# Choosing the experts of the early batches with the eight-highest instruction, in two parts spread over more steps

## The chip, the cores and the metric

One NeuronCore of a Trainium2 chip runs the kernel. The metric is the device time in microseconds (us) of one execution. Engines are called TensorE (PE in the profile, PEld its weight loads), VectorE (DVE), ScalarE (ACT), GpSimd (POOL) and SyncE (SP, which issues most transfers).

## The reference

A transformer layer on 32 batches of 112 tokens with 256 channels. First x = x + tanh(g) * attention(layernorm(x), context), with 16 heads of 16 channels and a causal window. Then x = x + tanh(g') * ffn(layernorm(x)), where the ffn is a mixture of 32 experts. What matters here is how the experts are chosen:

```
h = gelu([x, six statistics of x] @ r1.T + b)      # 3584 tokens, 128 wide
probs = softmax(h @ r2.T)                          # 32 experts
topp, topi = top_k(probs, 2)                       # two per token, the lower index wins a tie
wnorm = topp / topp.sum()
score = where(expert is one of the two, probs, -inf)
idx = argsort(-score over the tokens)[:140]        # each expert takes its 140 best tokens
out[idx] += w * expert(x[idx])                     # and 16 adapters weighted alike
```

## The kernel before

**Groups and steps.** The attention runs in 8 groups (NG) of 4 batches (GB), T = 112 tokens each. Each group is a hand-written software pipeline of 16 steps (STEPS); a step is one unit of 4 heads of one batch. The function `group` exists once per engine, and its arguments say which parts a pass holds: `front` (projections of the next group), `own` (the scores of this group) and `prev` (what is left of the group before, and its layer norm and router input). `groups` calls it for the passes; the last two calls are body(7), with own and prev but no front, and body(8), with prev alone. Below, steps 0 to 15 are those of body(7), and steps 16 to 31 those of body(8).

**One pair of steps.** At an even step TensorE writes the scores of two units (L1366, L1371). VectorE takes the row maxima (L1241), ScalarE the exponentials of each unit (L1072), TensorE turns them (L1380), VectorE and ScalarE copy one unit each to SBUF (L1247, L1060), and TensorE multiplies with the values (`weigh`, L1399, at odd steps). Each batch also has its softmax denominators: a reciprocal (L1231), a spreading copy (L1079), two transposes (`turn_sums`, L1411), a copy (L1085), and the product that yields the attention of the batch (L1236, at steps 0, 4, 8, 12, 16 and 20). That product frees the bank for the next batch's `weigh`. Then come the output projection (item "O", L1331) and the residual (L1175). The steps of these are lags in a table (TURN, WEIGH, DENOM, SUMS, ATT); each engine executes its queue strictly in that written order, and semaphores join them.

**The router.** For each group of batches, the pass after it applies the second layer norm (L1199, step 8), makes statistics on VectorE (L1206 to L1222, steps 10 and 12) and on GpSimd (L961 to L966), turns the tokens (items "T", L1317), the statistics ("S", L1346) and multiplies with r1 ("H", L1350 and L1352). ScalarE stores the result in `hpre` (L1045).

**The early choices.** The 24 batches of groups 0 to 5 (EARLY) are chosen during body(7), in the room that the missing front leaves. ScalarE applies the gelu to six groups at step 0 (L448), with a load of another function table before and after. TensorE makes the logits (L486) of two groups each at steps 1, 2 and 6 (LOGITS), into bank BM[0], which holds 16 batches at a time. VectorE subtracts the row maximum (`shift_logits`, L528 and L529) for batches 0 to 15 at step 5 and for 16 to 23 at step 7 (SHIFTED), ScalarE takes one exponential of all 24 at step 8 (L1099), and `choose` (L532 to L563) follows on VectorE in ten parts, on all 24 batches, at steps 9 to 15 (CHOOSE). Each of its operations but a reciprocal reads 24 x 32 = 768 elements a partition. A maximum (L547), a comparison with it (L548), a product with the expert's rank (L550), a second maximum (L551) and a second comparison (L553) make one choice; L556 takes it out, and the same five make the second. Every operation waits for the one before through `link` (the helper `Chain`).

**The late ones.** Batches 24 to 27 get their gelu in body(8). After the attention (`routing_vector`, L578) the last 8 batches go through the same `shift_logits` and `choose` in one stretch, on 8 x 32 = 256 elements, with nothing else on VectorE; then TensorE turns the scores (L496), ScalarE copies them, and VectorE starts the search for each expert's 140th best score (L597 on). `token_weights` (L565) makes the experts' weights for the tokens, for the early ones at the last step of body(8).

**Keeping TensorE busy.** `keep_warm` (L406 to L409) issues products of 448 columns whose result nobody reads: 12, 18 and 2 of them at steps 7, 12 and 14 of body(8) (IDLE).

```
LOGITS = {1: (0, 1), 2: (2, 3), 6: (4, 5)}
CHOOSE = {9: (0, 1), 10: (2,), 11: (3,), 12: (4, 5), 13: (6,), 14: (7,), 15: (8, 9)}
```

Of the kernel before, what the change touches and what calls it, by code (L numbers as in the profile page):

```python
# [17 lines left out]
GB = 4  # L18
# [43 lines left out]
def table():  # L62

    t = np.zeros((128, TAB_COLS), np.float32)
    t[:, TAB["ident"]] = np.eye(128)
    half = DH // 2
    freq = (1.0 / 10000.0 ** (np.arange(half, dtype=np.float32) / half)).astype(np.float32)
    ang = np.arange(T, dtype=np.float32)[None, :] * freq[:, None]
    row = np.arange(128)
    t[:, TAB["cos"]] = np.cos(ang)[row % half]  # L70
    t[:, TAB["sin"]] = np.sin(ang)[row % half] * np.where(row % DH < half, -1.0, 1.0)[:, None]
    q = np.arange(T)
    t[:T, TAB["causal"]] = np.where(q[None, :] > q[:, None], -1e30, 0.0)
    t[:, TAB["rev"]] = NE - np.arange(NE)
    t[:, TAB["parity"]] = (row[:, None] // DH) % 2 == np.arange(2)[None, :]
    t[:, TAB["chunk"]] = (row[:, None] % NE) == (row[None, :] % NE)
    t[:, TAB["before"]] = t[:, TAB["chunk"]] * (row[:, None] < row[None, :])
    t[:, TAB["seek"]] = 1 + np.arange(PAD)
    t[:, TAB["first"]] = ((row // NE) * CHB * T - TOKENS)[:, None]
    t[:, TAB["share"]] = np.where(row == NST - 1, 1.0 / C, 1.0)[:, None]  # L80
    t[:, TAB["spare"]] = TOKENS + row[:, None] + HC * np.arange(2)[None, :]
    return t
# [86 lines left out]
GELU, GELU_TAIL, SHIFTED = 0, 5, (5, 7)  # L169
LOGITS = {1: (0, 1), 2: (2, 3), 6: (4, 5)}  # L170
CHOOSE = {9: (0, 1), 10: (2,), 11: (3,), 12: (4, 5), 13: (6,), 14: (7,), 15: (8, 9)}
# [46 lines left out]
def program(nc, d, ctx):  # L218
# [83 lines left out]
    prb, w0, w1, h1, h2 = (take(T, [NB, NE]) for _ in range(5))  # L302
    sc = take(T, [CHB, NCH, NE])
    sc_flat = sc.rearrange("p j c e -> p (j c e)")
    col = [take(T, [NB]) for _ in range(8)]
# [100 lines left out]
    def keep_warm(times, weights, data):  # L406

        for _ in range(times):
            nc.tensor.matmul(banks[BS[0]][0:T, 0:NT], weights, data, start=True, stop=True)  # L409
# [33 lines left out]
    EARLY = (NG - 2) * GB  # L443
    LATE = slice(EARLY, NB)

# [86 lines left out]
    def choose(dve, link, rows, part, count):  # L532

        n = rows.stop - rows.start
        c = [a[:, rows] for a in col]
        p, u, v = (a[:, rows, :] for a in (prb, w0, w1))
        rev = over_b(tab[0:T, TAB["rev"]], n)

        values, top, hit = (p, c[4], h1[:, rows, :]) if part < 5 else (u, c[5], h2[:, rows, :])
# [6 lines left out]
        elif part in (2, 6):  # L546
            link(nc.vector.tensor_reduce(top, values, X, ALU.max))  # L547
            link(nc.vector.tensor_tensor(v, values, over_e(top), ALU.is_equal))  # L548
        elif part in (3, 7):
            link(nc.vector.tensor_tensor(v, v, rev, ALU.mult))  # L550
            link(nc.vector.tensor_reduce(c[3], v, X, ALU.max))  # L551
        elif part in (4, 8):
            link(nc.vector.tensor_tensor(hit, v, over_e(c[3]), ALU.is_equal))  # L553
        elif part == 5:

            link(nc.vector.scalar_tensor_tensor(u, h1[:, rows, :], -2.0, p, ALU.mult, ALU.add))  # L556
        elif part == 9:

            link(nc.vector.tensor_tensor(v, h1[:, rows, :], h2[:, rows, :], ALU.add))
            for chunk in range(rows.start // CHB, rows.stop // CHB):  # L560
# [4 lines left out]
    def token_weights(link, rows):  # L565


        c = [a[:, rows] for a in col]
        link(nc.vector.tensor_tensor(c[6], c[4], c[5], ALU.add))
        link(nc.vector.reciprocal(c[7], c[6]))  # L570
        link(nc.vector.tensor_scalar(c[7], c[7], gates[0:T, 2:3], None, ALU.mult))
        nc.vector.tensor_tensor(c[4], c[4], c[7], ALU.mult)
        link(nc.vector.tensor_tensor(c[5], c[5], c[7], ALU.mult))
        nc.vector.tensor_tensor(prb[:, rows, :], h1[:, rows, :], over_e(c[4]), ALU.mult)
        link(nc.vector.tensor_tensor(w1[:, rows, :], h2[:, rows, :], over_e(c[5]), ALU.mult))
        nc.vector.tensor_tensor(wts[:, rows, :], prb[:, rows, :], w1[:, rows, :], ALU.add).then_inc(s_wts, 1)

    def routing_vector(dve, link):  # L578
# [9 lines left out]
        for part in range(10):  # L588
            choose(dve, link, LATE, part, 2)
# [410 lines left out]
    def _(act):  # L1000
# [53 lines left out]
        def group(g, par, front, own, prev, _=1):  # L1054
            for s in range(STEPS):
# [41 lines left out]
                if own and not front and s == SHIFTED[-1] + 1:  # L1097
                    act.wait_ge(s_sub, 2)
                    nc.scalar.activation(w0[:, 0:EARLY, :], w0[:, 0:EARLY, :], ACT.Exp).then_inc(s_e, 1)  # L1099
# [9 lines left out]
    def _(dve):  # L1109
# [116 lines left out]
        def group(g, par, front, own, prev, _=1):  # L1226
            for s in range(STEPS):
# [49 lines left out]
                if own and not front:  # L1277
# [5 lines left out]
                    for h, rows in enumerate((slice(0, 16), slice(16, EARLY))):  # L1283
                        if s == SHIFTED[h]:
                            shift_logits(dve, link, rows, BM[0], rows.stop // GB)
                    for part in CHOOSE.get(s, ()):
                        choose(dve, link, slice(0, EARLY), part, 1)
# [16 lines left out]
    def _(pe):  # L1304
# [114 lines left out]

        def group(g, par, front, own, prev, loads=1):  # L1420
            for s in range(STEPS):
                if own and s % 2 == 0:
                    scores(g, par, s)
                for back, u in unit_at(s, TURN, own, prev):
                    turn(g - back, u)
                for back, u in unit_at(s, WEIGH, own, prev):
# [19 lines left out]
                for early in LOGITS.get(s, ()) if own and not front else ():  # L1446
                    if early == 0:
                        pe.wait_ge(s_mf[0], len(FRONT) * NG)
                    if early == GB:
                        pe.wait_ge(s_sub, 1)  # L1450
                    logits(pe, slice(early * GB, (early + 1) * GB), BM[0], early % GB * GB * NE)
# [50 lines left out]
```

## Time and profile before

| what | us |
|---|---|
| median of 3 runs (818.8 to 819.85) | 819.19 |
| the profiled execution | 815.54 |
| its span, first to last instruction | 813.7 |
| VectorE busy in the span | 513.5 |
| TensorE busy in the span | 678.9 |

The attention takes the span's first 443 us, the routing runs to 538 us, and the experts take the rest. The profile was taken in one execution; its times are from the start of the span. A mean under an engine's name is that of single instructions, which overlap a little on VectorE and ScalarE: the end of one is still running when the next starts.

### The profile page before, as it was taken

How to read it: one execution, taken by the hardware profiler on the slowest of the kernel's cores; microseconds unless marked ns; L12 is line 12 of the kernel's file. 1: busy time of each engine (PE TensorE's matmuls, PEld its weight loads, DVE VectorE, ACT ScalarE, POOL GpSimd, SP SyncE). 2: the span in 40 equal slices, each digit the busy share in tenths (PEclk: the TensorE clock that was granted, in tenths of full speed). 3: DMA queues.
4: the chain of work that ended last, by engine and by line, in shares of the span. 5: the costliest groups of instructions: out<-in, count | busy, mean ns of one | idle time of the engine just before them, and what ended most of it. 6: DMA issues, size and time to landing. Idle time of an engine off the chain costs nothing.

```text
span 813.7 us, 17427 instructions
## 1 busy us (share of the span) xinstructions
PE 678.9 (83%) x5196; PEld 533.9 (66%) x5196; DVE 513.5 (63%) x1322; ACT 393.3 (48%) x1589; POOL 323.6 (40%) x339
## 2 busy tenths in 40 slices
PE   6889999999999999989776111059999999999993
PEld 3556666666666666657543100049999999999992
DVE  5665677867777786745976988944444444444541
ACT  1467686777768676876632364003222222222220
POOL 3343452534444363431102000034656565656542
PEclk9999999999999999997888555569999999999997
DMA  5600020202002020100003500017888898998931
GB/s 161 236 1 24 25 69 2 69 25 68 23 23 70 1 68 23 46 1 23 24 1 87 157 0 0 0 32 214 271 247 274 247 264 253 266 262 241 268 70 14
DMA packets 57422, 84.44 MB, mean 104 GB/s; under 512 B 11282, under 2 KB 28304, under 8 KB 57360
## 3 DMA queue, kind: packets, MB, share of 16 engines
q1 hardware_dynamic: 47168, 73.04, 27.4%
q0 software_dynamic: 9216, 9.76, 7.6%
q10 hardware_dynamic: 976, 0.96, 0.4%
q8 instruction: 20, 0.33, 0.2%
q14 instruction: 42, 0.34, 0.1%
HBM read 71.04 MB, written 12.69 MB: 103 GB/s over the span
## 4 chain that ended last, share of the span: by engine, by line
PE 60%; DVE 19%; ACT 13%; issue 4%; DMA 1%; POOL 1%; ACTq 1%; DVEq 0%; POOLq 0%
PE pair L797 19%; PE bank L807 10%; ACT arena L1072 6%; PE pair L1371 6%; DVE arena L1241 5%; PE bank L1399 3%; PE pair L1380 3%; PE pair L1366 3%; DVE arena L658 3%; PE bank L1338 3%; PE bank L1326 2%; PE bank L1331 2%; PE bank L817 2%; ACT arena L477 2%; ACT arena L1027 1%
## 5 line engine op out<-in xcount | busy, mean ns | idle before, releaser
L1072 ACT ACTIVATE arena<-pair,arena 112x112 f32<-112x112 f32 x512 | 175.5, 365 | 81.1 <-DVE arena L1241 77.6
L797 PE MATMUL pair<-arena,we 128*128 128x140 f32 x1024 | 138.2, 283 | 0.8 <-ACT arena L718 0.6
L761 DVE SCALAR_TENSOR_TENSOR arena<-arena,pair 128x140 f32<-128x140 f32 x160 | 47.6, 298 | 137.0 <-ACT arena L726 137.0
L703 POOL DMA_INDIRECT rows_out<-arena,slot_row x64 | 94.4, 1475 | 91.0 <-DVE arena L750 75.2
L797 PEld LDWEIGHTS pair<-arena,we 128*128 128x128 f32 x1024 | 128.4, 190 | 1.9 <-issue 1.9
L726 ACT ACTIVATE arena<-pair 128x140 f32<-128x140 f32 x160 | 45.9, 287 | 147.4 <-PE pair L797 147.4
L694 POOL DMA_INDIRECT arena<-rows,slot_row x64 | 62.5, 977 | 121.2 <-issue 121.2
L1072 ACT ACTIVATION_READ_ACCUMULATOR arena<-pair,arena 112x1 f32 x512 | 109.9, 215 | 0.0
L1241 DVE TENSOR_REDUCE arena<-pair 112x8 f32<-112x896 f32 x64 | 69.2, 1081 | 25.7 <-PE pair L1371 25.0
L807 PE MATMUL bank<-arena,we 128*128 128x140 f32 x512 | 83.3, 286 | 0.0
L1380 PEld LDWEIGHTS pair<-tab,arena 112*112 112x112 f32 x512 | 53.2, 137 | 31.3 <-issue 28.5
L1380 PE MATMUL pair<-tab,arena 112*112 112x112 f32 x512 | 73.0, 270 | 0.0
L1399 PE MATMUL bank<-arena 112*32 112x112 f32 x1024 | 66.0, 273 | 6.4 <-DVE arena L1236 6.4
L807 PEld LDWEIGHTS bank<-arena,we 128*128 128x128 f32 x512 | 69.8, 190 | 0.0
L930 POOL TENSOR_TENSOR arena<-arena,tab 128x448 f32<-128x448 f32 x30 | 34.0, 1133 | 87.6 <-DVE we L1140 87.4
L1371 PE MATMUL pair<-arena 32*112 32x224 f32 x512 | 65.8, 374 | 0.0
L1399 PEld LDWEIGHTS bank<-arena 112*32 112x32 f32 x1024 | 49.7, 114 | 17.1 <-DVE arena L1236 6.8
L1326 PE MATMUL bank<-arena 128*128 128x448 f32 x128 | 58.6, 586 | 0.8 <-ACTq L1022 0.5
L1371 PEld LDWEIGHTS pair<-arena 32*112 32x112 f32 x512 | 40.8, 173 | 19.5 <-issue 18.0
L1366 PE MATMUL pair<-arena 112*112 112x448 bf16 x128 | 42.1, 375 | 7.0 <-ACT arena L1060 5.2
L766 DVE TENSOR_TENSOR arena<-arena,pair 128x140 f32<-128x140 f32 x128 | 38.4, 300 | 5.0
L1236 DVE TENSOR_TENSOR arena<-bank,arena 128x224 f32<-128x224 f32 x32 | 12.6, 393 | 43.3 <-ACT arena L1085 40.4
(192 smaller groups left out, 1183.7 us busy)
## 6 DMA issues: line engine op xcount, KB each, us to landing
we<-w_experts_in SPq DMA_DIRECT2D x192, 256.0 KB, 4.3
wa<-w_adapters_in SPq DMA_DIRECT2D x16, 384.0 KB, 5.7
arena<-ctx_in SPq DMA_DIRECT2D x8, 448.0 KB, 4.4
arena<-x_in SPq DMA_DIRECT2D x8, 448.0 KB, 3.8
rows_out<-arena SPq DMA_DIRECT2D x8, 448.0 KB, 3.3
rows<-arena SPq DMA_DIRECT2D x8, 448.0 KB, 3.4
arena<-rows,slot_row POOLq DMA_INDIRECT x64, 4.4
rows_out<-arena,slot_row POOLq DMA_INDIRECT x64
```

The lines of the kernel that those rows point to most:

```text
L694: nc.gpsimd.indirect_dma_start(xr[e % 4][:, h, :], None, d["rows"], bass.IndirectOffsetOnAxis(ap=slot_row[:, h, e:e + 1], axis=0)).then_in ...
L703: nc.gpsimd.indirect_dma_start(d["out"], bass.IndirectOffsetOnAxis(ap=slot_row[:, h, e:e + 1], axis=0), yr[e % 2][:, h, :], None, compute_ ...
L761: signal(dve, nc.vector.scalar_tensor_tensor(gs[m % 2], th[m % 2], 1.0, banks[m % 4][:, 0:CAP], ALU.add, ALU.mult), s_gs, n + 1)
L797: last = nc.tensor.matmul(banks[m % 4][:, part * CAP:(part + 1) * CAP], w[:, col0:col0 + 128], xet[j % 2][:, c, :], start=(c == 0), stop=( ...
L807: last = nc.tensor.matmul(banks[5 + o][:, 0:CAP], w[:, col0 + o * 128:col0 + (o + 1) * 128], hh[j % 2][:, k, :], start=(k == 0), stop=(k = ...
L1072: last = nc.scalar.activation(pr[s % 2][:, j, :], banks[BS[s % 4]][0:T, j * T:(j + 1) * T], ACT.Exp, bias=nmx[s // 2 % 2][:, s % 2, j:j + ...
L1241: nc.vector.tensor_reduce(nmx[s // 2 % 2], pairs[s // 2 % 2][0:T, :, 0:HU * T].rearrange("p u (h k) -> p u h k", h=HU), X, ALU.max, negate ...
L1326: last = nc.tensor.matmul(out[:, 0:NT], w[:, c, j * 128:(j + 1) * 128], src[:, c, :], start=(c == 0), stop=(c == 1))
L1366: nc.tensor.matmul(banks[BS[(s + i) % 4]][0:T, 0:HU * T], identb, causalb.unsqueeze(1).to_broadcast([T, HU, T]), start=True, stop=False)
L1371: last = nc.tensor.matmul(banks[BS[(s + i) % 4]][0:T, 2 * t * T:2 * (t + 1) * T], qt[par][rows, t, b * T:(b + 1) * T], kz[b % 2][rows, t, ...
L1380: last = nc.tensor.transpose(banks[BS[u % 4]][0:T, j * T:(j + 1) * T], pr[u % 2][:, j, :], ident[0:T, 0:T])
L1399: last = nc.tensor.matmul(banks[BO][rows, j // 2 * T:(j // 2 + 1) * T], vx[par][:, b * (NH // 2) + h // 2, 2 * (j % 2):2 * (j % 2) + 2, :] ...
```

## The change

The two highest of 32 values come from one instruction per batch, `nc.vector.max`, which writes the eight highest values of each partition in order (112 x 32 in, 112 x 8 out), into `top8` and `key8`. The choice goes in nine parts: sum and reciprocal (0), product (1), the eight highest of each batch's probabilities (2), their difference from the second highest (3), a key of 1 - e/32 where that isn't negative (4), plus 1 where it is positive (5), the eight highest of the keys (6), a comparison with the second of them (7), and the scores (8). `token_weights` multiplies the scores by one factor for each token.

The early batches go in two parts, 0 to 15 and 16 to 23, over steps 3 to 15 and 17 to 21; the tail of the choices runs in body(8). The logits of groups 4 and 5 move from step 6 to step 4. TensorE gets 7 unread products ahead of the logits at step 1, 2 ahead of those at step 4 and 4 at step 15, into bank BM[0].

```
-GELU, GELU_TAIL, SHIFTED = 0, 5, (5, 7)
-LOGITS = {1: (0, 1), 2: (2, 3), 6: (4, 5)}
-CHOOSE = {9: (0, 1), 10: (2,), 11: (3,), 12: (4, 5), 13: (6,), 14: (7,), 15: (8, 9)}
+GELU, GELU_TAIL = 0, 5
+LOGITS = {1: (0, 1), 2: (2, 3), 4: (4, 5)}
+EARLY_ROWS = (slice(0, 16), slice(16, 24))
+SHIFTED, RAISED = (3, 9), (4, 10)
+PARTS = 9
+CHOOSE = {5: ((0, 0), (0, 1)), 7: ((0, 2),), 9: ((0, 3),), 11: ((0, 4),), 13: ((0, 5),), 15: ((0, 6),),
+          16: ((0, 7), (0, 8)), 17: ((1, 0), (1, 1), (1, 2)), 19: ((1, 3), (1, 4), (1, 5)), 20: ((1, 6),),
+          21: ((1, 7), (1, 8))}
+IDLE_LOGITS, WITH_LOGITS = 7, 2
+IDLE_LAST = {15: 4}
...
         elif part in (2, 6):
-            link(nc.vector.tensor_reduce(top, values, X, ALU.max))
-            link(nc.vector.tensor_tensor(v, values, over_e(top), ALU.is_equal))
-        elif part in (3, 7):
-            link(nc.vector.tensor_tensor(v, v, rev, ALU.mult))
-            link(nc.vector.tensor_reduce(c[3], v, X, ALU.max))
-        elif part in (4, 8):
-            link(nc.vector.tensor_tensor(hit, v, over_e(c[3]), ALU.is_equal))
+            values, out = (prb, top8) if part == 2 else (w0, key8)
+            for b in range(rows.start, rows.stop):
+                last = nc.vector.max(out[:, b, :], values[:, b, :])
+            link(last)
+        elif part == 3:
+            link(nc.vector.tensor_tensor(v, p, second(top8), ALU.subtract))
+        elif part == 4:
+            link(nc.vector.scalar_tensor_tensor(u, v, 0.0, over_b(tab[0:T, TAB["rev"]], n), ALU.is_ge, ALU.mult))
         elif part == 5:
-            link(nc.vector.scalar_tensor_tensor(u, h1[:, rows, :], -2.0, p, ALU.mult, ALU.add))
-        elif part == 9:
-            link(nc.vector.tensor_tensor(v, h1[:, rows, :], h2[:, rows, :], ALU.add))
-            for chunk in range(rows.start // CHB, rows.stop // CHB):
+            link(nc.vector.scalar_tensor_tensor(u, v, 0.0, u, ALU.is_gt, ALU.add))
+        elif part == 7:
+            link(nc.vector.tensor_tensor(v, u, second(key8), ALU.is_ge))
+        elif part == 8:
+            for chunk in chunks:
                 at = slice(chunk * CHB, (chunk + 1) * CHB)
                 last = nc.vector.tensor_tensor(sc[:, :, chunk, :], prb[:, at, :], w1[:, at, :], ALU.mult)
             link(last)
...
     def token_weights(link, rows):
-        link(nc.vector.tensor_tensor(c[6], c[4], c[5], ALU.add))
-        link(nc.vector.reciprocal(c[7], c[6]))
-        link(nc.vector.tensor_scalar(c[7], c[7], gates[0:T, 2:3], None, ALU.mult))
-        nc.vector.tensor_tensor(c[4], c[4], c[7], ALU.mult)
-        link(nc.vector.tensor_tensor(c[5], c[5], c[7], ALU.mult))
-        nc.vector.tensor_tensor(prb[:, rows, :], h1[:, rows, :], over_e(c[4]), ALU.mult)
-        link(nc.vector.tensor_tensor(w1[:, rows, :], h2[:, rows, :], over_e(c[5]), ALU.mult))
-        nc.vector.tensor_tensor(wts[:, rows, :], prb[:, rows, :], w1[:, rows, :], ALU.add).then_inc(s_wts, 1)
+        link(nc.vector.tensor_tensor(c[0], top8[:, rows, 0], top8[:, rows, 1], ALU.add))
+        link(nc.vector.reciprocal(c[3], c[0]))
+        link(nc.vector.tensor_scalar(c[3], c[3], gates[0:T, 2:3], None, ALU.mult))
+        for chunk in range(rows.start // CHB, rows.stop // CHB):
+            at = slice(chunk * CHB, (chunk + 1) * CHB)
+            last = nc.vector.tensor_tensor(wts[:, at, :], sc[:, :, chunk, :], over_e(col[3][:, at]), ALU.mult)
+        last.then_inc(s_wts, 1)
...
-                if own and not front and s == SHIFTED[-1] + 1:
-                    act.wait_ge(s_sub, 2)
-                    nc.scalar.activation(w0[:, 0:EARLY, :], w0[:, 0:EARLY, :], ACT.Exp).then_inc(s_e, 1)
+                if own and not front and s in RAISED:
+                    h = RAISED.index(s)
+                    act.wait_ge(s_sub, h + 1)
+                    rows = EARLY_ROWS[h]
+                    nc.scalar.activation(w0[:, rows, :], w0[:, rows, :], ACT.Exp).then_inc(s_e, 1)
...
+        def fill_in(times):
+            keep_warm(times, identb, causalb.unsqueeze(1).to_broadcast([T, HU, T]), BM[0])
+
         def group(g, par, front, own, prev, loads=1):
             for s in range(STEPS):
                 if own and s % 2 == 0:
                     scores(g, par, s)
                 for back, u in unit_at(s, TURN, own, prev):
                     turn(g - back, u)
+                if own and not front and s in IDLE_LAST:
+                    pe.wait_ge(s_sub, 2)
+                    fill_in(IDLE_LAST[s])
...
                     if early == 0:
                         pe.wait_ge(s_mf[0], len(FRONT) * NG)
-                    if early == GB:
+                        fill_in(IDLE_LOGITS)
+                    elif early == GB:
                         pe.wait_ge(s_sub, 1)
+                        fill_in(WITH_LOGITS)
```

## Rows read from the trace of the kernel before

**Rows 1.** Busy time by stretch: PE, PEld, DVE, ACT, POOL, PEclk, DMA share, GB/s.
```profile
356.00:376.00 20.00, 17.46 (x118) 12.70 (x116) 4.59 (x8) 14.52 (x52) 0.93 (x1) 0.74 0.00 1
376.00:389.90 13.90, 12.91 (x123) 9.34 (x119) 11.11 (x26) 9.30 (x46) 2.21 (x3) 1.00 0.12 34
389.90:417.70 27.80, 19.28 (x135) 13.03 (x135) 26.48 (x48) 15.93 (x70) 3.56 (x6) 0.85 0.06 18
...
417.70:428.00 10.30, 8.87 (x54) 6.00 (x54) 4.36 (x14) 2.61 (x4) 0.13 (x1) 0.74 0.05 16
```

**Rows 2.** Chain of waits, steps 10 to 17: start, us, what.
```profile
397.87 0.96 DVE arena L547
...
417.71 0.40 DVE arena L1236
...
418.16 1.71 PE bank L1399 x16
```

**Rows 3.** VectorE's timeline, 386 to 428 us: start, us, engine, line, operation, shapes.
```profile
386.17 0.39 DVE L1236 TENSOR_TENSOR arena<-bank,arena 128x224 f32<-128x224 f32 x1 [0.97 <-ACT arena L1085]
...
392.37 1.03 DVE L1241 TENSOR_REDUCE arena<-pair 112x8 f32<-112x896 f32 x1
...
402.13 1.08 DVE L1241 TENSOR_REDUCE arena<-pair 112x8 f32<-112x896 f32 x1
...
410.53 1.03 DVE L1241 TENSOR_REDUCE arena<-pair 112x8 f32<-112x896 f32 x1
...
427.14 0.18 DVE L1191 BATCH_NORM_AGGREGATE arena<-arena 112x2 f32<-112x6 f32 x1
```

**Rows 4.** Groups of VectorE's instructions, shapes apart, whole span: busy, mean ns.
```profile
L547 DVE TENSOR_REDUCE arena<-arena 112x24 f32<-112x768 f32 x2 | 1.9, 953 | 0.1
L528 DVE TENSOR_REDUCE arena<-bank 112x16 f32<-112x512 f32 x1 | 0.7, 692 | 0.2 <-DVE arena L1187 0.2
L547 DVE TENSOR_REDUCE arena<-arena 112x8 f32<-112x256 f32 x2 | 0.8, 419 | 0.1
L1187 DVE BATCH_NORM_AGGREGATE arena<-arena 112x2 f32<-112x6 f32 x24 | 2.5, 161 | 1.2 <-DVE arena L1184 0.9
```

**Rows 5.** VectorE's timeline: three small independent instructions in a row.
```profile
379.09 0.31 DVE L1187 BATCH_NORM_AGGREGATE arena<-arena 112x2 f32<-112x6 f32 x3
```

**Rows 6.** TensorE's timeline in steps 1 to 4 and at step 12.
```profile
362.76 1.73 PE L486 MATMUL bank<-r2t,hpre 128*112 128x32 f32 x16 [1.83 <-ACT hpre L448]
...
365.97 1.84 PE L1371 MATMUL pair<-arena 32*112 32x224 f32 x8
...
368.52 3.06 PE L486 MATMUL bank<-r2t,hpre 128*112 128x32 f32 x16
...
375.25 1.01 PE L1371 MATMUL pair<-arena 32*112 32x224 f32 x8
...
390.25 0.40 PE L1366 MATMUL pair<-arena 112*112 112x448 bf16 x1 [1.26 <-ACT arena L1060]
```

**Rows 7.** Busy time by microsecond, columns of rows 1: where the granted clock changes.
```profile
365.00:366.00 1.00, 0.58 (x3) 0.20 (x3) 0.00 (x0) 0.98 (x2) 0.00 (x0) 0.50 0.00 0
...
375.00:376.00 1.00, 1.00 (x9) 0.63 (x8) 0.39 (x1) 0.00 (x0) 0.00 (x0) 0.90 0.00 0
...
392.00:393.00 1.00, 1.00 (x10) 0.99 (x8) 0.96 (x3) 0.86 (x2) 0.00 (x0) 0.63 0.07 24
...
436.00:437.00 1.00, 1.00 (x5) 0.57 (x4) 1.00 (x7) 0.00 (x0) 0.33 (x1) 0.68 0.00 0
```

**Rows 8.** Timelines of ScalarE and TensorE from 414 us.
```profile
414.97 0.39 ACT L1085 COPY arena<-bank 128x224 f32<-128x224 f32 x1
...
433.25 5.26 PE L409 MATMUL pair<-arena 112*112 112x448 bf16 x18
```

**Rows 9.** Chain of waits in the choice of the late batches.
```profile
447.08 0.43 DVE arena L542
...
454.25 1.77 PE pair L496 x8
```

More of the change, by code:

```diff
@@ L73, in table @@
     t[:T, TAB["causal"]] = np.where(q[None, :] > q[:, None], -1e30, 0.0)
-    t[:, TAB["rev"]] = NE - np.arange(NE)
+    t[:, TAB["rev"]] = 1 - np.arange(NE) / NE
     t[:, TAB["parity"]] = (row[:, None] // DH) % 2 == np.arange(2)[None, :]
@@ L301, in program @@
     used[0] = 0
-    prb, w0, w1, h1, h2 = (take(T, [NB, NE]) for _ in range(5))
+    prb, w0, w1 = (take(T, [NB, NE]) for _ in range(3))
+    top8, key8 = (take(T, [NB, 8]) for _ in range(2))
     sc = take(T, [CHB, NCH, NE])
     sc_flat = sc.rearrange("p j c e -> p (j c e)")
-    col = [take(T, [NB]) for _ in range(8)]
+    col = [take(T, [NB]) for _ in range(4)]
     assert used[0] <= free_early
@@ L404, in groups, with keep_warm @@
         body(NG, 0, False, False, True)
-    def keep_warm(times, weights, data):
+    def keep_warm(times, weights, data, bank=BS[0]):
         for _ in range(times):
-            nc.tensor.matmul(banks[BS[0]][0:T, 0:NT], weights, data, start=True, stop=True)
+            nc.tensor.matmul(banks[bank][0:T, 0:NT], weights, data, start=True, stop=True)
     PIECE = 512
@@ L443, in program @@
     EARLY = (NG - 2) * GB
+    assert EARLY_ROWS[-1].stop == EARLY
     LATE = slice(EARLY, NB)
@@ L536, in choose @@
         p, u, v = (a[:, rows, :] for a in (prb, w0, w1))
-        rev = over_b(tab[0:T, TAB["rev"]], n)
-        values, top, hit = (p, c[4], h1[:, rows, :]) if part < 5 else (u, c[5], h2[:, rows, :])
+        second = lambda a: over_e(a[:, rows, 1])
+        chunks = range(rows.start // CHB, rows.stop // CHB)
         if part == 0:
@@ L587, in routing_vector @@
         shift_logits(dve, link, LATE, BS[0], EARLY // GB + 1)
-        for part in range(10):
-            choose(dve, link, LATE, part, 2)
+        for part in range(PARTS):
+            choose(dve, link, LATE, part, 3)
         dve.sem_inc(s_scr, 1)
@@ L1282, in group @@
                             dve.wait_ge(done, value)
[L1283 to L1287, printed above, removed]
+                    if s in SHIFTED:
+                        rows = EARLY_ROWS[SHIFTED.index(s)]
+                        shift_logits(dve, link, rows, BM[0], rows.stop // GB)
+                if not front:
+                    for h, part in CHOOSE.get(s if own else s + STEPS, ()):
+                        choose(dve, link, EARLY_ROWS[h], part, h + 1)
         dve.wait_ge(s_gate, 1)
```

## The prediction

> **What bounds the kernel now.** I read the stretches first. From 389.9 to 417.7 us, steps 9 to 15, VectorE is busy 26.5 of 27.8 us and TensorE 19.3 [rows 1]: the only part of the attention in which VectorE is the bound. The chain of waits says the same: from 397.87 to 417.71 us it runs through nothing but VectorE, over the choice (L547 to L562), to the product L1236 on which TensorE's `weigh` starts at 418.16 [rows 2]. The rhythm shows what that costs. The maxima L1241 of steps 10, 12 and 14 begin at 392.37, 402.13 and 410.53 [rows 3], 9.8 and 8.4 us apart; ahead of the choice steps 4 and 8 took some 5 us a pair (376 to 389.9 us, TensorE busy 12.9 of 13.9 [rows 1]).
>
> A second loss lies in steps 1 to 4. ScalarE has the gelus, TensorE waits 1.83 us, and its granted clock falls to 0.50 (1.2 GHz) at 365 us and is back at 375 [rows 6, 7]. There eight products of the scores take 1.84 us and later 1.01, and 16 logits 3.06 against 1.73 just before [rows 6].
>
> The third place is the choice of the last 8 batches, 447.08 to 454.25 us, all of it on VectorE, and TensorE waits for its end [rows 9].
>
> **Prices on VectorE.** An operation on 768, 512 and 256 elements takes 0.95, 0.69 and 0.42 us [rows 4]; with the 0.04 us between linked ones I take 0.99, 0.73 and 0.46. The two ends give 1.04 ns an element. No row has the eight-highest instruction. It reads 32 elements, 0.033 us at that rate. Three small independent instructions took 0.31 us together at 0.161 each, so 0.075 from start to start [rows 4, 5]. I take 0.11 us for each, since the eight highest of the batches are independent too. The lower end is 0.08 (only the spacing). The upper end is a small instruction's full 0.161 [rows 4], the 0.033 and nearly nothing of overlap, 0.20. So eight take 0.9 us with their link, sixteen 1.8; at the upper end 1.6 and 3.2.
>
> The row speaks for overlap. The Trainium skill, VectorE: DVE Perf Modes, in its section on the TRN2 errata, speaks against the change: each instruction on SBUF pays a fixed latency, whatever its size, and work should be cut in tiles of 512 elements or more; it has measured about 150 cycles of it. By that an estimate of the instruction is 0.19 us and the sum below is that of the second rival. That the latency isn't paid in full between independent instructions is what the three small ones show here.
>
> **The change, part by part.**
>
> 1. *Steps 8 to 16.* Before, the choice holds fourteen operations on 768 elements (14 x 0.99), a reciprocal (about 0.3) and three score products on 256 (together 1.1): 15.3 us. After, steps 9 to 15 hold the shift of 8 batches (2 x 0.46), three operations on 16 batches (3 x 0.73) and sixteen eight-highest (1.8): 4.9 us. L1236 of step 8 begins at 386.17 and that of step 16 at 417.71 [rows 2, 3], 31.5 us. VectorE alone would need 31.5 - 15.3 + 4.9 = 21.1 us. But other work now ends last. Step by step: the maxima of step 10 at 391.4 (5 us behind those of step 8, TensorE's pace). Those of step 12 at 397.8: other work filled 392.37 to 397.87, 5.5 us [rows 2, 3], and 0.73 and the reciprocal or product ahead of the maxima join it. Those of step 14 at 403.0: from 8.4 us go four operations, 4.0, and 0.73 comes. From there the chain of exponentials, copy, transposes and L1085 took 410.53 to 415.36 in the trace [rows 3, 8], 4.8 us. It gives L1236 at 408.0 instead of 417.71: **-9.7 us**. Late next are ScalarE's L1085, and VectorE's sixteen, which end at 406.8; they have 1.2 us to spare. The four unread products at step 15 stand ahead of `weigh` and H, 4 x 0.19 us (part 6). TensorE would reach the sums' transposes at about 406.7, and ScalarE copies them at 407.6. Hidden; without that cover 0.8 us.
>
> 2. *Steps 3 to 8.* The first shift goes to step 3, where VectorE is idle (busy 4.6 of 20 us [rows 1]); queued behind its wait for the logits is only step 4's product, which comes later. Sum, reciprocal and product at step 5 take 1.7 us where the shift took 1.6. The logits of step 4, with two unread products, put 2.1 us in front of `weigh` and O, and the maxima of step 6 some 1.5 us later; step 6 loses as much, and with ScalarE's exponential of all 24 batches out of step 8 the maxima of step 10 come at 391.4 all the same, not at 392.37. Cost nothing beyond part 1. Without that cover it would be 1.5 us.
>
> 3. *Steps 16 to 22.* New on VectorE: 0.73 + 0.76, then 0.69 + 0.46 + 0.9, then 3 x 0.46, then 0.9, then 0.96: 6.8 us. In this stretch it was busy 4.4 of 10.3 us [rows 1], so 0.9 us don't fit, and since the new work stands in the queue ahead of the reciprocal of step 18 and of the product of step 20, another 1.2 us of its idle time is of no use: L1191, which ends the second layer norm's statistics at 427.3 [rows 3], comes 11.7 us after step 16's product instead of 9.6. **+2.1 us.** GpSimd's root and the following norm wait for it.
>
> 4. *The late choice.* Before 7.17 us [rows 9]. After: seven operations on 256 elements (7 x 0.46), a reciprocal (0.23) and twice 0.9: 5.25 us. **-1.9 us.** `token_weights` gets shorter, beside the transposes and copies; nothing. No transfer is added or moved past a queue.
>
> 5. *TensorE's clock in steps 1 to 4.* Seven unread products take 1.3 us of the 1.83 it waits [rows 6]. From 365.97 to 376.26 us, 10.3 us, TensorE works without a gap, nearly all at the lower clock; by the pairs 1.84 to 1.01 and 3.06 to 1.73 [rows 6] it would be 0.56 as long, 4.5 us less, if the clock stayed at 2.4 GHz. I take 0: at 392 us it fell behind a wait of only 1.26 us with TensorE busy on both sides [rows 6, 7], and the rest of the wait and the short logits remain. Ends: +0.8 (the seven at the lower clock), -4.5.
>
> 6. *The 18 unread products of step 28* end last at their place: 5.26 us from 433.25 [rows 8], with the clock rising at 436.7 [rows 7], so nine at each level: 9 x a + 9 x 2a gives a = 0.195 us. All at 1.2 GHz they are 7.0, all at 2.4 GHz 3.5. I take no change; ends +1.7 and -1.7.
>
> Sum: -9.7 + 2.1 - 1.9 = -9.5 us. Against the profiled execution's 815.54 that is 806.0. The median of the runs stands 3.65 us above that execution; I carry the difference over: 819.19 - 9.5 = **809.7 us**.
>
> **The rivals.**
>
> *A, the clock holds in steps 1 to 4* (part 5 at its end): 809.7 - 4.5 = 805.2. For it, two thirds of the wait are filled. Against it, the fall at 392.
>
> *B, the eight-highest instruction costs 0.20 us.* The late choice gives back 2 x 0.7; steps 17 and 20 the same 1.4; step 7 has 3.2 us instead of 1.8 ahead of step 8 and delays it 1.3; step 15 eats its 1.2 and 0.2 more: 809.7 + 4.3 = 814.0. The page named above gives this.
>
> *C, TensorE takes the bound over.* With VectorE relieved, steps 9 to 16 keep TensorE at it nearly all the time (19.3 us busy [rows 1] plus the fill); if a pair takes 5.5 us instead of 5.1 and the 18 products run at 1.2 GHz: 3 x 0.4 + 1.7, 812.6.
>
> *D, slower: the eight-highest instruction runs on its own at 0.35 us.* Place: 16 late, 16 in steps 17 and 20, 16 in step 7, 16 in step 15. Each 0.1 us more costs 5 to 6 us, so from 0.28 us on the gain of 9.5 is gone; at 0.35 the time is 823. The smallest reduction and statistics read above take under 0.2 beyond their elements [rows 4], so this is unlikely.
>
> *E, the relief doesn't arrive*, since another wait of these steps was as late as VectorE: only the late choice gains, 817.3. Against it, TensorE waits for L1236 in both places.
>
> **How the numbers follow.** Forecast 52%, A 18%, B 12%, C 12%, D 3%, E 3%. The forecast's own range is 808 to 811.5. The range that holds 8 in 10 reaches from just under A to just over B and leaves out D, E and the far ends: 804.8 to 814.5. About 0.2% is what a measurement of this kernel can tell from no change. Faster than that are the forecast, A, B, C and E: 0.95; slower D: 0.03; the rest within it, 0.02.
>
> **What the changed profile would show.** Part 1: the maxima of steps 10, 12 and 14 some 5 to 6.5 us apart, and L1236 of step 16 led by ScalarE's L1085, 8 to 10 us earlier against step 8's. Part 3: the same lines 11 to 12 us from step 16's product to the last aggregate. Part 4: 5.2 us from the late sum to the transposes, and eight instructions in 0.9 us. Part 5: granted clock 0.50 for some 10 us behind the gelus. Wrong it would be with eight of them in over 1.3 us, with gaps over 7 us still between those maxima, or with a clock of 1.00 from 365 to 375 us.

## The result and the profile after

| | us |
|---|---|
| before, median of 18 runs (814.95 to 822.39) | 818.86 |
| changed, median of 18 runs (808.84 to 819.33) | 815.87 |
| ratio, with its 95% interval | 0.9959 (0.994 to 0.9978) |
| changed, the profiled execution | 816.06 |
| its span | 814.3 |

The change gains 3 us by the medians, 1.8 to 4.9 us by the interval of the ratio, not 9.5. Two things in the table are worth more than its median: the changed kernel's quickest runs are 6 us below the quickest before, and its runs scatter by 10 us. Single executions of three kernels below stand apart with another granted clock (818.52 and 1391.63 us of two changed kernels, 1186.83 us of the kernel before); the medians and ratios leave them out.

The page of the changed kernel: share of the span by engine, and TensorE's granted clock in 40 slices.

```profile
span 814.3 us, 17505 instructions
PE 682.5 (84%) x5209; PEld 536.7 (66%) x5209; DVE 508.7 (62%) x1371; ACT 394.2 (48%) x1590; POOL 323.4 (40%) x339
...
PEclk8999999999999999995887555579999999999997
```

VectorE lost 4.8 us of work. The clock stands at its lower level in the nineteenth slice (366 to 387 us, from step 2 on), where before it was at 7 tenths.

VectorE's timeline of the changed kernel, the maxima of steps 0, 4, 6, 8, 10, 12 and 14 (L1254), the product of steps 8 and 16 (L1249), the eight-highest instructions (L562), and the aggregate that ends the tail (L1204). Start, us, engine, line, operation, idle time before.

```profile
356.59 1.09 DVE L1254 TENSOR_REDUCE arena<-pair 112x8 f32<-112x896 f32 x1 [0.49 <-PE pair L1385]
...
375.60 1.09 DVE L1254 TENSOR_REDUCE arena<-pair 112x8 f32<-112x896 f32 x1 [1.78 <-PE pair L1385]
...
385.88 1.09 DVE L1254 TENSOR_REDUCE arena<-pair 112x8 f32<-112x896 f32 x1 [5.08 <-PE pair L1385]
...
388.95 1.59 DVE L562 MAX8 arena<-arena 112x8 f32<-112x32 f32 x16 [0.15 <-DVE arena L1204]
390.88 0.39 DVE L1249 TENSOR_TENSOR arena<-bank,arena 128x224 f32<-128x224 f32 x1 [0.34 <-DVE arena L562]
391.19 1.08 DVE L1254 TENSOR_REDUCE arena<-pair 112x8 f32<-112x896 f32 x1
...
396.05 1.03 DVE L1254 TENSOR_REDUCE arena<-pair 112x8 f32<-112x896 f32 x1
...
402.58 1.08 DVE L1254 TENSOR_REDUCE arena<-pair 112x8 f32<-112x896 f32 x1
...
408.74 1.09 DVE L1254 TENSOR_REDUCE arena<-pair 112x8 f32<-112x896 f32 x1 [0.91 <-PE pair L1385]
...
414.27 0.39 DVE L1249 TENSOR_TENSOR arena<-bank,arena 128x224 f32<-128x224 f32 x1 [1.78 <-issue]
...
426.07 0.18 DVE L1204 BATCH_NORM_AGGREGATE arena<-arena 112x2 f32<-112x6 f32 x1
```

The timeline shows two opposite things. From step 8's product to step 16's it is now 23.4 us, before 31.5 [rows 2, 3]: the gaps of 9.8 and 8.4 us are 6.5 and 6.2. But the maxima of step 6 come 10.3 us behind those of step 4, with VectorE idle for 5.08 us and waiting for TensorE. Before, these were 5 us apart, and step 8 began 28.3 us behind step 0 instead of 34.6. The kernel before, the maxima of steps 0, 4, 6 and 8:

```profile
358.15 1.09 DVE L1241 TENSOR_REDUCE arena<-pair 112x8 f32<-112x896 f32 x1 [0.50 <-PE pair L1371]
...
376.34 1.09 DVE L1241 TENSOR_REDUCE arena<-pair 112x8 f32<-112x896 f32 x1 [0.95 <-PE pair L1371]
381.31 1.03 DVE L1241 TENSOR_REDUCE arena<-pair 112x8 f32<-112x896 f32 x1
...
386.47 1.08 DVE L1241 TENSOR_REDUCE arena<-pair 112x8 f32<-112x896 f32 x1
```

TensorE's timeline in that hole, steps 1 to 6.

```profile
359.21 1.50 PE L420 MATMUL bank<-arena 112*112 112x448 bf16 x7
361.11 1.76 PE L498 MATMUL bank<-r2t,hpre 128*112 128x32 f32 x16 [0.40 <-ACT hpre L460]
...
364.41 1.84 PE L1385 MATMUL pair<-arena 32*112 32x224 f32 x8
366.18 0.99 PE L1394 MATMUL pair<-tab,arena 112*112 112x112 f32 x4
366.96 3.06 PE L498 MATMUL bank<-r2t,hpre 128*112 128x32 f32 x16
...
373.69 1.84 PE L1385 MATMUL pair<-arena 32*112 32x224 f32 x8
375.46 0.99 PE L1394 MATMUL pair<-tab,arena 112*112 112x112 f32 x4
376.25 0.95 PE L420 MATMUL bank<-arena 112*112 112x448 bf16 x2
377.00 3.06 PE L498 MATMUL bank<-r2t,hpre 128*112 128x32 f32 x16
...
382.41 2.05 PE L1345 MATMUL bank<-arena 128*112 128x256 f32 x4
```

And busy time by stretch with the granted clock (behind the length: PE, PEld, DVE, ACT, POOL, then PEclk).

```profile
355.00:362.00 7.00, 6.60 (x55) 4.70 (x55) 2.18 (x4) 5.46 (x19) 0.00 (x0) 1.00 0.00 1
...
364.00:384.00 20.00, 20.00 (x107) 15.73 (x108) 8.60 (x18) 10.40 (x46) 0.94 (x1) 0.50 0.00 1
...
401.00:408.00 7.00, 6.73 (x38) 4.64 (x38) 6.56 (x16) 3.97 (x20) 2.70 (x5) 0.53 0.01 2
```

The clock fell at 364 us in spite of the seven unread products, and it stayed at 1.2 GHz for 20 us; before it was 10 [rows 7]. The moved logits (377.00, 3.06 us where they take 1.7 at full clock) lie in the middle of it, on TensorE's path, 20 of 20 us busy.

The end of the late choice, VectorE's timeline.

```profile
449.42 0.84 DVE L562 MAX8 arena<-arena 112x8 f32<-112x32 f32 x8
...
456.53 0.63 DVE L608 TENSOR_SCALAR arena<-arena 128x896 int32<-128x896 int32 x1 [4.06 <-DMA arena<-search_in]
```

SyncE's timeline in the same stretch: start, us, queue, line, operation.

```profile
450.28 0.65 SPq L910 DMA_DIRECT2D arena<-search_in  x1
452.50 0.34 SPq L912 DMA_DIRECT2D rows<-wts  x1
```

The choice itself is as short as forecast, 446.01 to 451.25 us. But the first digit of the search (L608) waits 4.06 us for the search table, which SyncE issues behind 13 loads of weights at 450.28 and which lands 6.2 us later. From the end of the attention (VectorE's first MEMSET behind it, at 442.15 and before at 443.22) to that digit it is 14.4 us, before 13.9. From the sum that opens the choice (L555, at 446.01, before L542 at 447.08) to the digit it is 10.5 us, before 10.0.

### The profile page after: what moved, and what is told of

It is laid out like the page before. It is cut to its first block, busy times and chain, and to the rows that moved or that the text cites. A ratio compares the mean times of both kernels' runs of the same rounds, so it can differ in the third digit from the quotient of the medians.

```text
span 814.3 us, 17505 instructions
## 1 busy us (share of the span) xinstructions
PE 682.5 (84%) x5209; PEld 536.7 (66%) x5209; DVE 508.7 (62%) x1371; ACT 394.2 (48%) x1590; POOL 323.4 (40%) x339
## 4 chain that ended last, share of the span: by engine, by line
PE 61%; DVE 17%; ACT 12%; issue 4%; DMA 2%; SPq 1%; POOL 1%; ACTq 0%; DVEq 0%; POOLq 0%
PE pair L808 19%; PE bank L818 10%; PE pair L1385 6%; ACT arena L1083 6%; DVE arena L1254 4%; PE pair L1394 3%; PE bank L1413 3%; PE pair L1380 3%; DVE arena L669 3%; PE bank L1352 3%; PE bank L1345 2%; PE bank L1340 2%; PE bank L828 2%; PE bank L1364 2%; PE bank L1331 1%
## 5 line engine op out<-in xcount | busy, mean ns | idle before, releaser
L1254 DVE TENSOR_REDUCE arena<-pair 112x8 f32<-112x896 f32 x64 | 69.4, 1084 | 30.8 <-PE pair L1385 30.0
L1413 PE MATMUL bank<-arena 112*32 112x112 f32 x1024 | 64.2, 268 | 0.3 <-DVE arena L1249 0.3
L1340 PE MATMUL bank<-arena 128*128 128x448 f32 x128 | 56.1, 565 | 0.6 <-ACTq L1033 0.3
L1260 DVE COPY arena<-pair 112x448 f32<-112x448 f32 x64 | 39.4, 616 | 0.4 <-PE pair L1394 0.4
```

Of the source, the lines that this page charges most:

```text
L1254: nc.vector.tensor_reduce(nmx[s // 2 % 2], pairs[s // 2 % 2][0:T, :, 0:HU * T].rearrange("p u (h k) -> p u h k", h=HU), X, ALU.max, negate ...
L1340: last = nc.tensor.matmul(out[:, 0:NT], w[:, c, j * 128:(j + 1) * 128], src[:, c, :], start=(c == 0), stop=(c == 1))
L1413: last = nc.tensor.matmul(banks[BO][rows, j // 2 * T:(j // 2 + 1) * T], vx[par][:, b * (NH // 2) + h // 2, 2 * (j % 2):2 * (j % 2) + 2, :] ...
```

## The experiments

Each kernel is compared with the kernel before on the same chip. The medians of the kernel before differ by up to 3 us between chips, so the ratios are what compares; behind each stands its 95% interval. "Steps 0 to 8" is the time from the maxima of step 0 to those of step 8 in the profile. Each profile is of one execution only, and it isn't always a typical one.

**Each suspected loss alone.**

The table's transfer first:

```
-        load_pair(1, 1)
         nc.sync.dma_start(srt, d["search"]).then_inc(s_dig, 16)
+        load_pair(1, 1)
```

> The changed kernel, with the transfer of the search table issued ahead of the 13 expert loads at the end of the attention instead of behind them. Theory (the late choice's gain is eaten by this transfer): the table lands before 450 us of the profile instead of 456.5, the first digit follows ScalarE's copies at about 2.4 us behind the place where it stood (456.53 becomes about 454.1), and the median falls by 2 to 2.5 us below that of the changed kernel, to 813.5. Rival (SyncE's loads are what matters, or another wait is as late): no change, 815.9, and VectorE's first digit still at 14.4 us behind the attention's end.

Measured: median 812.12, ratio 0.993 (0.9905 to 0.9955), against 0.9959 for the changed kernel, some 2.4 us better, though the two intervals overlap. The first digit now follows ScalarE's copy, 12.7 us behind the attention's end instead of 14.4, and 8.15 us behind the sum that opens the choice instead of 10.5.

> The kernel before with the same swap of the two transfers. Theory: there the table lands 0.2 us ahead of ScalarE's copy, so nothing is gained: 818.9, ratio 1.000 within 0.002. Rival (the order of the transfers is worth something by itself, whatever the choice costs): 816.5, ratio 0.997.

Measured: 817.96, ratio 1.0007 (0.9987 to 1.0027). Alone the order of the transfers gains nothing: from the sum to the digit it is 10.0 us as without it. The table became a bound only when the choice got shorter than it.

The logits back:

```
-LOGITS = {1: (0, 1), 2: (2, 3), 4: (4, 5)}
+LOGITS = {1: (0, 1), 2: (2, 3), 6: (4, 5)}
```

> The changed kernel with the logits of groups 4 and 5 back at step 6; all else as changed. Theory (the logits at step 4 fall into the time in which the clock is low after the gelus, and keep it low for steps 4 and 5): granted clock back at 1.00 some 10 us after its fall and not 20, maxima of step 8 about 29 us behind those of step 0 instead of 34.6, median 810 to 813, and fewer runs above 816. Rival (the clock's course is chance, and the place of the logits costs nothing): 815.9 with the same spread.

Measured: 810.68 (807.77 to 812.47), ratio 0.9931 (0.9911 to 0.995), 2.3 us better than the changed kernel; the two intervals just touch. The profile fell on the quickest of the six runs. Steps 0 to 8 take 28.6 us instead of 34.6, and the clock is back some 10 us behind its fall:

```profile
363.00:373.00 10.00, 9.40 (x53) 7.46 (x53) 3.40 (x5) 7.12 (x30) 0.94 (x1) 0.51 0.01 2
373.00:375.00 2.00, 2.00 (x16) 1.25 (x15) 0.87 (x2) 0.14 (x1) 0.00 (x0) 0.90 0.00 0
375.00:400.00 25.00, 22.06 (x204) 15.70 (x204) 22.90 (x67) 19.32 (x91) 5.52 (x9) 1.00 0.13 38
```

With the clock up, the rest of the forecast stands in this kernel's timelines: step 8's product at 384.57, step 16's at 406.40, 21.8 us, and the last aggregate at 418.11. ScalarE's copy (L1096) ends at 406.31, just ahead of step 16's product.

```profile
384.57 0.39 DVE L1249 TENSOR_TENSOR arena<-bank,arena 128x224 f32<-128x224 f32 x1 [0.34 <-DVE arena L562]
...
405.92 0.39 ACT L1096 COPY arena<-bank 128x224 f32<-128x224 f32 x1
406.40 0.39 DVE L1249 TENSOR_TENSOR arena<-bank,arena 128x224 f32<-128x224 f32 x1 [1.25 <-issue]
...
418.11 0.18 DVE L1204 BATCH_NORM_AGGREGATE arena<-arena 112x2 f32<-112x6 f32 x1
```

No unread products (`IDLE_LOGITS, WITH_LOGITS = 0, 0` and `IDLE_LAST = {}`):

> The changed kernel without its 13 unread products (7, 2 and 4). Theory (they do not hold the clock: in the profile it fell at 364 us in spite of them): 815.9, within 1 us, clock low from 364 us on for as long as with them. Rival (they hold it in the quick half of the runs, 808.8 to 812.4): no run below 813, median 818.

Measured: 809.78 (807.35 to 814.47), ratio 0.9934 (0.9905 to 0.9962). Neither expectation: by the median it gains as much as moving the logits back (the interval still holds the changed kernel's 0.9959), and in the profile, again of the quickest run, the clock was back after 10 us although the logits stood at step 4. So the loss may lie in the unread products, or in them and the moved logits together, as well as in the logits, and this profile already shows that logits at step 4 don't always mean a long low stretch.

**The mends together, beside the changed kernel again.**

> The changed kernel, nothing edited, beside the three below on one chip, as their measure. Theory (the course of the clock in steps 1 to 6 makes two kinds of runs): ratio to before 0.996 again, runs from some 3 us below the median to 3 us above, and a mean clock of the run that goes with its time.

Measured: 815.15 (808.62 to 817.96), ratio 0.9958 (0.9931 to 0.9985), the first measurement again. Its profile fell on its quickest run: clock low from 365.5 to 372.3 us only, steps 0 to 8 in 28.3 us. Taken together the changed kernel's 30 runs go from 808.62 to 819.33, 12 of them below 813.5, and their time goes with the mean granted clock, at a correlation of -0.94 (0.914 at 808.84, 0.898 at 819.33). That clock is a mean over the whole execution, and the kernel before has the same correlation on this chip (-0.95), so it doesn't show that steps 1 to 6 are what differs.

> The changed kernel with both mends: the logits of groups 4 and 5 at step 6, and the search table's transfer ahead of the expert loads. Theory (two separate losses): the gains add, 2.3 us and 2.4 us below the changed kernel of the same chip, ratio to before 0.990, which is the forecast's 9.5 us less about 1. Rival (one of the two stands for the other): ratio 0.993 like either alone.

Measured: 811.24 (807.37 to 814.43), ratio 0.991 (0.988 to 0.994). Against the changed kernel on the same chip (0.9958) that is 3.9 us, clear of the noise. The theory's 0.990 and the rival's 0.993 both lie in the interval, so whether the two gains add in full isn't shown.

> The run before it (both mends) without the 13 unread products. Theory (they do nothing where the logits are at step 6, since the clock falls at the same place with and without them): the same within 0.1%. Rival (each unread product before step 4 stands in TensorE's way while its clock is low, as the run without them at step 4 hinted): 1 to 2 us faster still, ratio 0.988. Other rival (they hold the clock in some runs): slower by 1 to 2 us.

Measured: 809.4 (807.42 to 811.75), ratio 0.9898 (0.9862 to 0.9934). The interval holds the run before it and the first rival's 0.988; no use of the 13 products shows here.

Four more, in TensorE's second wait of step 1:

```
                     logits(pe, slice(early * GB, (early + 1) * GB), BM[0], early % GB * GB * NE)
+                    if early == 1:
+                        fill_in(4, BM[2])
```

> Both mends, and 4 more unread products right behind the logits of step 1, in the second wait, into bank BM[2]. Theory (the clock falls since TensorE waits and then has only narrow logits; with the second wait filled too it may stay): if it holds, steps 0 to 4 take 14 us instead of 18.2 and the ratio goes to 0.985. Rival (the narrow products of 32 columns and scores of 32 rows are what lets it fall): it falls at the same place, ratio 0.990.

Measured: 805.7 (803.68 to 806.06), ratio 0.9841 (0.9807 to 0.9875). That is 5.5 us better than without the four. In the profile the clock stays: steps 0 to 4 take 14.0 us, steps 0 to 8 24.4. TensorE's timeline:

```profile
361.28 1.50 PE L420 MATMUL bank<-arena 112*112 112x448 bf16 x7
363.18 1.76 PE L498 MATMUL bank<-r2t,hpre 128*112 128x32 f32 x16 [0.40 <-ACT hpre L460]
364.77 0.95 PE L420 MATMUL bank<-arena 112*112 112x448 bf16 x4
365.56 0.77 PE L1380 MATMUL pair<-arena 112*112 112x448 bf16 x2
366.26 1.01 PE L1385 MATMUL pair<-arena 32*112 32x224 f32 x8
...
367.63 1.67 PE L498 MATMUL bank<-r2t,hpre 128*112 128x32 f32 x16
```

Its stretches, with the granted clock behind the five engines:

```profile
362.00:373.00 11.00, 10.58 (x95) 7.94 (x92) 4.06 (x7) 10.27 (x36) 0.94 (x1) 1.00 0.01 2
373.00:383.00 10.00, 9.11 (x87) 6.70 (x86) 8.82 (x34) 7.52 (x37) 2.00 (x3) 1.00 0.16 46
```

The products stand in a wait of 0.78 us; the scores behind them still start with ScalarE's copy, and take 1.01 us instead of 1.84.

**What each part is worth.**

> The quickest version so far (both mends, 7 and 4 unread products at step 1), with the logits of groups 4 and 5 back at step 4. Theory (their place costs only where the clock is low): the clock stays, and the ratio is 0.984 to 0.986, as with step 6. Rival (they cost by their order, 2.1 us in front of the scores of step 6): ratio 0.987 or more.

Measured: 806.47 (804.59 to 808.91, five runs), ratio 0.9888 (0.986 to 0.9917) of the kernel before. In the profile the clock stays up, and steps 0 to 8 take 25.1 us instead of 24.4: the order of the logits costs 0.7 us at full clock, where the changed kernel's profile was 6 us longer than with the logits at step 6. The ratio lies on the rival's side (0.987 or more), and the theory's 0.984 to 0.986 only touches the interval, so the runs as a whole leave room for a larger cost than 0.7 us.

The kernel before with the same 7 and 4 products and nothing else:

> The kernel before with nothing but 7 and 4 unread products at step 1. Theory (the low clock of steps 1 to 4 is a loss of its own, 4.2 us from the scores of step 2 to those of step 4, and it passes on): clock at 1.00 through steps 1 to 4, ratio 0.995. Rival (VectorE, the bound from step 9 on, swallows it): ratio 0.999.

Measured: 811.51, ratio 0.9937 (0.9913 to 0.996). The low clock of steps 1 to 4 was a loss of its own, by the medians larger than the gain of the whole change as made (5 us against 3; the intervals overlap). In the profile steps 0 to 4 take 14.0 us; there the clock falls later, from 379 to 389 us, and that execution took 816.41.

The eight-highest instruction for the late batches alone, in the kernel before:

> The kernel before with the eight-highest instruction for the late 8 batches alone; the early ones and the schedule as before. Theory (the search table's transfer is as late as the old choice): the choice takes 5.2 us instead of 7.2, but the first digit starts only 0.2 us or so sooner behind the attention's end, ratio 0.9995. Rival (my forecast's -1.9 us arrives): ratio 0.9977.

Measured: 816.73, ratio 0.9992 (0.9969 to 1.0015). The choice is 1.9 us shorter, and nothing measurable comes of it, but the interval holds the rival too. In the profile the digit waits 2.29 us for the table and starts 13.3 us behind the attention's end.

> The same with the search table's transfer ahead of the expert loads. Theory: the 1.9 us arrive, the first digit starts 12.0 us behind the attention's end instead of 13.9, ratio 0.9977. Rival (something else is as late as the table): ratio 1.000.

Measured: 816.71, ratio 1.0002 (0.9986 to 1.0018). The first digit starts 12.7 us behind the attention's end, in the profile of the kernel before with the table first 14.6. So the 1.9 us reach the digit; the absolute 12.0 and 13.9 us of the expectation don't recur, since in this profile the logits ahead of the choice ran at the lower clock. Yet the median has none of it, and the interval leaves out the theory's 0.9977.

**The same questions in the quickest version.**

> The quickest version again (logits at step 6, table first, 7 and 4 unread products at step 1), as the measure of the three beside it on one chip: ratio 0.984 to 0.987, scatter of the runs under 4 us.

Measured: 805.19 (802.94 to 808.57), ratio 0.9867 (0.9836 to 0.9898). The ratio is as expected, the scatter isn't: 5.6 us, not under 4.

> That version with the old ten-part choice and the old weights for the last 8 batches. Theory (the late choice's 1.9 us arrive once the table doesn't wait): 1.9 us slower than the quickest version, median difference 1.5 to 2.5 us. Rival (they are lost again before the experts, in the clock's rise or elsewhere): within 0.5 us of it.

Measured: 805.78 (803.46 to 811.69), ratio 0.9879 (0.9842 to 0.9916). The difference of medians is 0.6 us, near the rival's 0.5, but each interval reaches some 3 us to either side and settles nothing between 0 and 1.9 us. The profiles show both sides. The digit starts 1.9 us later with the old choice (14.6 against 12.7), but the experts' first 24 products take 3.10 us, as in the kernel before, and 4.76 with the new choice, since the clock is up 1.2 us ahead of them in the one and 3.4 us behind their start in the other. TensorE's timeline at the experts' start, with the old late choice:

```profile
533.79 3.10 PE L848 MATMUL pair<-arena,we 128*128 128x140 f32 x24 [0.57 <-ACT arena L769]
```

The same with the new one, in the profile of the first quickest version:

```profile
532.40 4.76 PE L808 MATMUL pair<-arena,we 128*128 128x140 f32 x24 [0.57 <-issue]
```

> That version without the 2 unread products at step 4 and the 4 at step 15. Theory (they fill waits in which the clock doesn't fall anyway, and steps 12 to 16 hang on ScalarE): the same within 0.5 us. Rival (the four at step 15 keep the clock): 1 to 2 us slower, with the clock at 0.50 in steps 15 to 18.

Measured: 805.0 (801.32 to 811.11), ratio 0.9878 (0.9837 to 0.992). The same by the median, with a scatter of 9.8 us; in the profile the clock in steps 4 to 15 didn't fall without them. (The two products go with the logits, so in this version they stood at step 6.)

> That version without the 7 unread products at step 1, with the 4 behind the logits alone. Theory (both waits have to be filled): the clock falls some 5 to 9 us behind the maxima of step 0 again, 4 us slower. Rival (the second wait alone decides): as quick as the quickest version.

Measured: 810.22 (807.82 to 812.16), ratio 0.9928 (0.99 to 0.9957), 5 us slower. The clock falls and stays low for 20 us:

```profile
363.00:383.00 20.00, 20.00 (x105) 14.85 (x104) 8.54 (x18) 12.22 (x50) 0.93 (x1) 0.50 0.00 1
```

Both waits of step 1 have to be filled. The change filled the first alone, which shows no gain. The profiles of all kernels agree: in the six with both waits filled the clock stays up through steps 1 to 4, and in the other twelve it falls.

**How long the low stretch lasts.** This is the stretch behind step 0 in those twelve profiles, sorted by the place of the logits of groups 4 and 5. "First" and "second" are the unread products in the two waits of step 1.

| kernel | logits at | first, second | clock low, us | steps 0 to 8, us |
|---|---|---|---|---|
| changed | 4 | 7, 0 | 20 | 34.6 |
| changed, table first | 4 | 7, 0 | 17 | 33.0 |
| changed, measured again | 4 | 7, 0 | 7 | 28.3 |
| changed, no unread products | 4 | 0, 0 | 10 | 29.1 |
| changed, logits back | 6 | 7, 0 | 10 | 28.6 |
| both mends | 6 | 7, 0 | 10 | 28.5 |
| both mends, no unread products | 6 | 0, 0 | 14 | 29.5 |
| quickest version without the seven | 6 | 0, 4 | 20 | 32.6 |
| before | 6 | 0, 0 | 10 | 28.3 |
| before, table first | 6 | 0, 0 | 10 | 28.2 |
| before, new late choice | 6 | 0, 0 | 17 | 30.3 |
| before, new late choice, table first | 6 | 0, 0 | 10 | 28.3 |

One kernel has 7 and 20 us, and stretches of 17 and 20 us also come with the logits at step 6. So the profiles don't show that the moved logits lengthen the stretch. They do show what the logits cost inside it: in a stretch of 17 or 20 us steps 0 to 8 are 2.7 and 2.0 us longer with the logits at step 4 than at step 6, in one of 10 us some 0.5 to 0.9 us, and at full clock 0.7 us.

## Why the prediction was wrong, point by point

**Prices: right.** Eight of the new instructions took 0.84 us and sixteen 1.59, against 0.9 and 1.8 with their link. Independent ones follow each other every 0.1 us. The Trainium skill (VectorE: DVE Perf Modes, section on the TRN2 errata) has a fixed latency of about 150 cycles for each instruction; an estimate with it in full each time is 1.5 us for eight. The trace, with 0.84 us, disagrees for a row of independent small instructions.

**Part 1, -9.7 us: right where the clock was up.** The kernel with the logits at step 6 has 21.8 us between the two products, the number forecast, and ScalarE's copy ends last, 0.1 us ahead of the second, as forecast. The changed kernel has 21.8 us too in its second profile; in the first it has 23.4, where the clock was at 0.53 from 401 to 408 us.

**Part 2, "cost nothing beyond part 1": wrong, the step that failed.** I moved the logits to step 4 with two unread products and priced their order at full clock, with 1.5 us as the bound, to be made good by step 10. At full clock it is 0.7 us in the profiles. But my own part 5 had the clock low from 365 to 375 us, and step 4 begins at its end: if the stretch lasts longer than the 10 us of the one profile I had, the moved logits and their two products cost nearly twice as much, as does all of TensorE's work beside them. With the logits back the ratio falls by 0.28%, 2.3 us, and with both mends by 3.9 us. In the changed kernel's first profile steps 0 to 8 are 6.3 us longer than before, but most of that is the long low stretch itself. I treated its length as given; it is 7 to 20 us in the profiles, and why it is long in one execution and short in the next stays open, as does the share of the unread products: by the median, leaving them out gained as much as moving the logits back.

**Part 3, +2.1 us: right in size.** It was 2.4 in the changed kernel (414.27 to 426.25 us, before 9.6) and 2.3 with the logits at step 6. No run shows what it costs the whole.

**Part 4, -1.9 us: right for the choice, wrong for the path, the second step that failed.** 5.24 us instead of 7.17. What I wrote of the transfers, that none is moved past a queue, was true and beside the point: one was already as late as the old choice. In the kernel before, the table landed at 456.85 us (issued at 451.45, 5.4 us on its way), 0.2 us ahead of the end of ScalarE's copy at 457.01, and the wait was invisible, because that copy ended last. In the changed kernel the wait comes last, and its size varies: from the sum that opens the choice to the digit the four profiles with the table behind the loads have 10.5, 9.1, 8.4 and 10.3 us, those with the table first 8.15 us. So the wait takes 0.2 to 2.4 of the gain. Rival E named a wait as late as VectorE, but only for the early part. Putting the table first brought 0.3% in the changed kernel, not clear of the noise by itself. That the late choice's 1.9 us arrive is shown to the first digit only; behind it the experts' start differs with the clock by 1.7 us and more, and the two runs made for it give 0.0 and 0.6 us. Whether that is chance or follows from the earlier arrival stays open.

**Part 5, no gain from the seven: right**, with the reason I gave (the rest of the wait remains): with the rest filled the clock held in every profile, and steps 0 to 4 were 4.2 us shorter, on the kernel before too, near rival A's 4.5. The stretch itself wasn't always the 10 us forecast. **Part 6: right**, 5.27 us.

The sum with both mends gave ratio 0.991, 7.4 us (4.9 to 9.8) of the 9.5, without any clock kept; with it 0.984 and 0.987. The two mends are 3.9 of the missing 6.5 us, and the forecast lies within the interval of what is left.

## What to carry to other kernels

Before work is moved in a queue, look at the granted clock in the stretch it is moved into: TensorE's work costs nearly double there (16 logits 3.06 us against 1.67), and one profile doesn't tell how long such a stretch lasts (here 7 to 20 us). When a critical stage gets shorter, list everything its successor waits for with its time of arrival, transfers too, since a wait that was hidden by 0.2 us appears in no list of waits. And where a fall of the clock has two waits ahead of it, fill both: here filling either one alone gained nothing.

## What the runs showed of the hardware

- MAX8 on 112 x 32 values: 0.84 us for 8 and 1.59 for 16 independent ones, from start of the first to the end of the last.
- One program, one chip: 10 us of scatter in 18 runs go with the granted clock, correlation -0.96. With both waits of step 1 filled, 12 runs of one program on two chips lie between 802.94 and 808.57, but 6 of the same without the unread products of later steps between 801.32 and 811.11.
- Behind the same code the clock stayed at 1.2 GHz for 7 us in one profile of the changed kernel and for 20 in another, with TensorE 20 of 20 us busy in the latter.
- The experts' first 24 products took 3.10, 4.76 or 5.94 us in profiles of kernels that hold the same code there, by when the clock rose.
- The quickest version is the change with the logits at step 6, the table's transfer first, and 7 and 4 unread products at step 1: median 805.6 of 12 runs, ratios 0.9841 and 0.9867 to the kernel before.
